# The sync engine reads the places of a pair of blocks ahead of its wait for their buffer, and the last sequence's results get buffers of their own

## The reference

```python
x = x + _layernorm(_L0_attn_ref(_layernorm(x), W_q, W_k, W_v, W_o))
x = x + _layernorm(_L0_ffn_ref(_layernorm(x), gate_w, gate_bias, Wg, Wu, Wd, Ws_g, Ws_u, Ws_d))

# in _L0_ffn_ref, x being its (normed) input:
hg = jnp.einsum('nh,eih->nei', xf, Wg)
hu = jnp.einsum('nh,eih->nei', xf, Wu)
act = jax.nn.silu(hg) * hu
y = jnp.einsum('nei,ne,ehi->nh', act, cw, Wd)      # cw: gates, 4 of 16 nonzero per token
shared = jax.nn.silu(xf @ Ws_g.T) * (xf @ Ws_u.T) @ Ws_d.T
return x + (y + shared)
```

## Time and profile before

| | us |
|---|---|
| median of 3 runs | 1031.69 (1030.8 to 1032.27) |
| the profiled execution | 1031.85 |
| its span | 1030.0 |
| TensorE busy | 830.4 (81%) |
| DVE busy | 654.9 (64%) |
| ACT busy | 452.2 (44%) |
| POOL busy | 434.8 (42%) |
| chain that ended last | PE 27%, DVE 12%, DMA 6%, issue 5%, SPq 4% |
| mean granted TensorE clock | 0.90 of full speed |

### The profile page before, as it was taken

One profiled execution on the slowest core, in us unless ns is written; L12 is line 12 of the kernel. 1 busy time (PEld: TensorE's weight loads), 2 busy tenths in 40 slices (PEclk: granted clock), 3 DMA queues, 4 the chain that ended last, 5 costly groups with the idle time before them and its releaser, 6 DMA issues.

```text
span 1030.0 us, 20612 instructions
## 1 busy us (share of the span) xinstructions
PE 830.4 (81%) x6580; PEld 610.5 (59%) x6580; DVE 654.9 (64%) x1906; ACT 452.2 (44%) x763; POOL 434.8 (42%) x416
## 2 busy tenths in 40 slices
PE   3449887896898798698796887799988999988763
PEld 3326454564565465466464555688877788777521
DVE  4375758687687787777777694554553333877543
ACT  2115544553544455363464555555444455444300
POOL 4431203115425425424522424467567655655610
PEclk9758989899898899898898898899999999998977
DMA  4475744334444443533559422354556667988663
GB/s 164 118 189 149 226 109 126 81 84 138 127 112 116 130 123 118 136 102 98 157 156 304 138 88 91 109 177 150 175 172 217 201 168 265 337 302 305 237 234 123
DMA packets 89175, 168.72 MB, mean 164 GB/s; under 512 B 14704, under 2 KB 56688, under 8 KB 88816
## 3 DMA queue, kind: packets, MB, share of 16 engines
q1 hardware_dynamic: 75248, 128.85, 43.7%
q0 software_dynamic: 13824, 38.55, 9.9%
HBM read 90.15 MB, written 76.68 MB: 162 GB/s over the span
## 4 chain that ended last, share of the span: by engine, by line
PE 27%; DVE 12%; DMA 6%; issue 5%; SPq 4%; POOL 3%; ACT 2%; DVEq 0%; ACTq 0%; POOLq 0%
PE ring L1480 7%; PE ring L1501 3%; DVE nmax L781 3%; DMA xg<-sorted_rows 2%; PE ring L1259 2%; DMA ykt<-expert_rows 2%; PE ring L1466 2%; PE ring L1261 2%; PE ring L1260 2%; POOL expert_rows L699 2%; PE ring L1380 2%; SPq L592 2%; PE ring L1337 1%; DMA expert_rows<-ys,dest 1%; SPq L593 1%
## 5 line engine op out<-in xcount | busy, mean ns | idle before, releaser
L1189 ACT ACTIVATE prob<-ring 128x1024 f32<-128x1024 f32 (+1 forms) x192 | 167.4, 880 | 208.1 <-PE ring L1328 207.8
L781 DVE TENSOR_REDUCE nmax<-ring 128x2 f32<-128x1024 f32 (+3 forms) x256 | 200.8, 818 | 43.5 <-PE ring L1310 41.6
L699 POOL DMA_INDIRECT expert_rows<-ys,dest x160 | 157.7, 985 | 96.9 <-ACT ys L1143 40.5
L691 POOL DMA_INDIRECT sorted_rows<-xr,idx_all x128 | 131.0, 1023 | 79.7 <-DVE xr L940 46.6
L1480 PE MATMUL ring<-we,xh 128*128 x640 | 155.1, 386 | 0.0
L1480 PEld LDWEIGHTS ring<-we,xh 128*128 128x128 f32 x640 | 118.3, 195 | 13.3
L1003 DVE SCALAR_TENSOR_TENSOR sl<-sl,got,ring 128x128 f32<-128x128 f32 x160 | 48.3, 344 | 104.1 <-ACT sl L1241 103.8
L1322 PE MATMUL ring<-maskt_b,halves_b 64*128 64x128 bf16 (+2 forms) x768 | 57.2, 229 | 63.6 <-DVE nmax L781 37.0
L669 POOL TENSOR_TENSOR rot<-rot 128x512 f32<-128x512 f32 x16 | 20.4, 1278 | 204.6 <-DVE rot L773 204.6
L1322 PEld LDWEIGHTS ring<-maskt_b,halves_b 64*128 64x128 bf16 x768 | 22.5, 96 | 133.2 <-DVE nmax L781 53.7
L1337 PE MATMUL ring<-prob,v_sb 128*32 128x512 f32 (+3 forms) x1024 | 97.9, 481 | 1.7 <-ACT prob L1189 1.7
(11 more groups left out here) (194 smaller groups left out, 1673.7 us busy)
## 6 DMA issues: line engine op xcount, KB each, us to landing
xg<-sorted_rows SPq DMA_DIRECT2D x160, 134.0 KB, 2.5
parts<-part SPq DMA_DIRECT2D x32, 512.0 KB, 5.8
ykt<-expert_rows SPq DMA_DIRECT2D x16, 1024.0 KB, 9.4
k_st<-parts SPq DMA_DIRECT2D x64, 128.0 KB, 3.6
q_st<-parts SPq DMA_DIRECT2D x64, 128.0 KB, 3.5
we<-w_exp SPq DMA_DIRECT2D x1, 6144.0 KB, 21.9
sorted_rows<-zeros SPq DMA_DIRECT2D x2, 2144.0 KB, 12.0
sorted_rows<-zeros SPq DMA_DIRECT2D x32, 134.0 KB
```

What stands on the lines that cost most here:

```text
L691: pool.indirect_dma_start(out=xs[group_of(s)], out_offset=bass.IndirectOffsetOnAxis(ap=idx_all[:, s, t, k:k + 1], axis=0), in_=xr[:, s % 2 ...
L699: pool.indirect_dma_start(out=yk, out_offset=bass.IndirectOffsetOnAxis(ap=dest[:, j % 8, b:b + 1], axis=0), in_=ys[:, j % NYS, b, :], in_o ...
L781: dve.tensor_reduce(nmax[:, Q % 2, :, pp, qb], slot[:, :, col:col + (qb + 1) * P], AX.X, ALU.max, negate=True).then_inc(s_max, 1)
L1189: act_e.activation(prob[:, u % 2, 2 * half:2 * half + 2, 0:width], slot[:, :, 0:width], ACT.Exp, scale=SCALE).then_inc(s_exp, 1)
```

## The change

Two things. In `load_block` both value loads of a pair come ahead of the waits for the buffer; the two loads of `xg` stay behind them. And the last sequence (7) gets places of its own, `ykt_last`, `zt_last` and `x1t_last`, in the space of `w_hi`, `w_lo`, `h_hi` and `h_lo`; semaphores are added for them. `home(s)` is the number of a sequence's place, `turn(s)` the how many-th use of it this is, `back(s)` gives its three tiles. In group 1 all residual loads (CZ 5, 6, 7) and then all six loads of parts (CL) come at the head of the steps.

```diff
@@ def sums(g)
     halves = [(s, h) for s in range(first, end) for h in range(2)]
+    if end == B:
+
+        steps = [("CZ", g, s) for s in range(first, end)] + [("CL", g, *half) for half in halves]
+        for i, (s, h) in enumerate(halves):
+            steps += [("CA", g, s, h), ("CS", g, s, h)]
+            if i:
+                steps.append(("CN", g, *halves[i - 1]))
+        return steps + [("CN", g, *halves[-1])]
@@ places
+        cursor[0] = w_low
+        ykt_last = place("ykt_last", [P, NT, TOPK, D])
+        zt_last = place("zt_last", [P, NT, D])
+        x1t_last = place("x1t_last", [P, NT, D])
+        assert cursor[0] <= w_high
@@ semaphores
-        s_cl = [sem(f"parts_back{i}") for i in range(4)]
-        s_cz = [sem(f"residuals_back{i}") for i in range(2)]
+        s_cl = [sem(f"parts_back{i}") for i in range(6)]
+        s_cz = [sem(f"residuals_back{i}") for i in range(3)]
-        s_out = [sem(f"out_stored{i}") for i in range(2)]
+        s_out = [sem(f"out_stored{i}") for i in range(3)]
@@ which place
+        def home(s):
+
+            return 2 if s == B - 1 else s % 2
+
+        def turn(s):
+
+            return 1 if s == B - 1 else s // 2 + 1
+
+        def back(s):
+
+            if s == B - 1:
+                return ykt_last, zt_last, x1t_last
+            return ykt[:, s % 2, :, :, :], zt[:, s % 2, :, :], x1t[:, s % 2, :, :]
@@ SP: load_block
+                row = [sp.value_load(tab[blk:blk + 1, g, 0:1], min_val=0, max_val=E * REGION + (DUMMIES - 1) * P)
+                       for blk in (2 * i, 2 * i + 1)]
                 if j >= NXG:
                     sp.wait_ge(s_t1, j - NXG + 1)
                     sp.wait_ge(s_dest, j - NXG + 1)
                 for b in range(2):
-                    blk = 2 * i + b
-                    row = sp.value_load(tab[blk:blk + 1, g, 0:1], min_val=0, max_val=E * REGION + (DUMMIES - 1) * P)
-                    sp.dma_start(xg[:, j % NXG, b, :], xs[g][bass.ds(row, P), :]).then_inc(s_xg[j % NXG], 16)
+                    sp.dma_start(xg[:, j % NXG, b, :], xs[g][bass.ds(row[b], P), :]).then_inc(s_xg[j % NXG], 16)
@@ SP: load_residuals, load_sums
-                if s >= 2:
-                    sp.wait_ge(s_out[s % 2], 32 * (s // 2))
+                _, z_home, x1_home = back(s)
+                if turn(s) > 1:
+                    sp.wait_ge(s_out[home(s)], 32 * (turn(s) - 1))
...
-                if s >= 2:
+                if turn(s) > 1:
                     sp.wait_ge(s_cn, N_OUT * (2 * (s - 2) + h + 1))
...
-                sp.dma_start(dst, per_token).then_inc(s_cl[2 * (s % 2) + h], 16)
+                dst = back(s)[0][:, NHALF * h:NHALF * h + NHALF, :, :].rearrange("p t k d -> p t (k d)")
+                sp.dma_start(dst, per_token).then_inc(s_cl[2 * home(s) + h], 16)
@@ PE: sum_results
-                pe.wait_ge(s_cl[2 * (s % 2) + h], 16 * (s // 2 + 1))
+                pe.wait_ge(s_cl[2 * home(s) + h], 16 * turn(s))
```

More of the change, by code:

```diff
@@ L590, in load_block @@
                 for b in range(2):
[L591 to L593 removed]
+                    sp.dma_start(xg[:, j % NXG, b, :], xs[g][bass.ds(row[b], P), :]).then_inc(s_xg[j % NXG], 16)
             def load_residuals(s):
[L596 to L597 removed]
+                _, z_home, x1_home = back(s)
+                if turn(s) > 1:
+                    sp.wait_ge(s_out[home(s)], 32 * (turn(s) - 1))
                 sp.wait_ge(s_zst, 16 * (s + 1))
                 sp.wait_ge(s_x1st, 16 * (s + 1))
[L600 to L601 removed]
+                sp.dma_start(z_home[:, :, :], packed(z_dram[s])).then_inc(s_cz[home(s)], 16)
+                sp.dma_start(x1_home[:, :, :], packed(x1_dram[s])).then_inc(s_cz[home(s)], 16)
             def load_sums(s, h):
@@ L617, in store_out @@
                 tiles = slice(NHALF * h, NHALF * h + NHALF)
-                sp.dma_start(rows(out[s])[:, tiles, :], zt[:, s % 2, tiles, :]).then_inc(s_out[s % 2], 16)
+                sp.dma_start(rows(out[s])[:, tiles, :], back(s)[1][:, tiles, :]).then_inc(s_out[home(s)], 16)
             load_x(0)
@@ L655, in _ @@
                     store_out(st[2], st[3])
-            for par in range(2):
-                sp.wait_ge(s_out[par], 32 * (B // 2))
+            for place_of in range(3):
+                sp.wait_ge(s_out[place_of], 32 * max(turn(s) for s in range(B) if home(s) == place_of))
         @block.gpsimd
@@ L1007, in final_sums @@
                 tiles = slice(NHALF * h, NHALF * h + NHALF)
-                y = ykt[:, s % 2, tiles, :, :]
+                y, z_home = back(s)[0][:, tiles, :, :], back(s)[1]
                 done = sums_before(s, h)
@@ L1011, in final_sums @@
                     if h == 0:
-                        dve.wait_ge(s_cz[s % 2], 32 * (s // 2 + 1))
+                        dve.wait_ge(s_cz[home(s)], 32 * turn(s))
                     n = 2 * (s - SHARED) + h
@@ L1031, in final_statistics @@
                 for t in range(NHALF * h, NHALF * h + NHALF):
-                    dve.bn_stats(st3[:, t, :], ykt[:, s % 2, t, 0, :]).then_inc(s_cst, 1)
+                    dve.bn_stats(st3[:, t, :], back(s)[0][:, t, 0, :]).then_inc(s_cst, 1)
                 for n in range(NHALF):
@@ L1044, in final_rows @@
                 dve.wait_ge(s_cr, 2 * s + h + 1)
+                y_home, z_home, x1_home = back(s)
                 for t in range(NHALF * h, NHALF * h + NHALF):
-                    dve.tensor_scalar(zt[:, s % 2, t, :], ykt[:, s % 2, t, 0, :], mv3[:, t, 0:1], rstd3[:, t:t + 1],
+                    dve.tensor_scalar(z_home[:, t, :], y_home[:, t, 0, :], mv3[:, t, 0:1], rstd3[:, t:t + 1],
                                       ALU.subtract, ALU.mult).then_inc(s_cn, 1)
                 dve.wait_ge(s_cn, done + NHALF)
-                dve.tensor_tensor(zt[:, s % 2, tiles, :], zt[:, s % 2, tiles, :], x1t[:, s % 2, tiles, :],
-                                  ALU.add).then_inc(s_cn, 1)
+                dve.tensor_tensor(z_home[:, tiles, :], z_home[:, tiles, :], x1_home[:, tiles, :], ALU.add).then_inc(s_cn, 1)
             dve.memset(zeros[:, :], 0.0).then_inc(s_init, 1)
@@ L1379, in sum_results @@
                 for k in range(TOPK):
-                    last = pe.matmul(ring[2][:, n % 2, :], ident, ykt[:, s % 2, NHALF * h:NHALF * h + NHALF, k, :],
+                    last = pe.matmul(ring[2][:, n % 2, :], ident, back(s)[0][:, NHALF * h:NHALF * h + NHALF, k, :],
                                      start=k == 0, stop=k == TOPK - 1)
```

5 lines of the change are left out of this document (3 added, 2 removed).

## The result

| | before | after |
|---|---|---|
| median of the runs, us | 1031.98 (1030.8 to 1033.94, 4 runs) | 1022.78 (1020.89 to 1023.75, 4 runs) |
| ratio after / before | | 0.9907, 95% interval 0.9885 to 0.9929 |
| profiled execution, us | 1031.85 | 1020.89 |
| its span, us | 1030.0 | 1019.1 |

The change saves 9.2 us of the medians, 0.9%. The forecast was 1020.8: 2 us too low, and inside its range.

The account below looks back on a forecast made before the run. The prediction saw the end bound by a detour for sequence 7, and SP late with xg pairs at two sites. Terms -1.15 - 1.2 - 10.0 + 1.5 = -10.85 gave a median of 1020.8 us, range 1018.0 to 1025.3.

Parts of the forecast that it names:

- The tail: Kernel's end: sequence 7's own home and six part loads in a row bring the last DVE sum 10.0 us sooner.
- The pads: Group 1's pads, 767 to 808: SP starts 1.15 us sooner, TensorE's xg stalls fall from 5.6 to 4.4; -1.15.
- the first sums: Behind the dest wait at 859.7: pairs and part loads come 1.15 us sooner, shortening DVE and TensorE waits; -1.2.
- Elsewhere 0: Remaining places, including TensorE's three xg waits in 860 to 980: the value loads gain nothing there; 0.
- three stalls of 9.3 us: TensorE's xg waits in 860 to 980, behind output stores or large loads: move along with what precedes them; 0.
- Rival 2: Value loads buy nothing: slower issues or growing later xg stalls take their gain; -8.5, 1023.2 us; chance 0.23.
- The residuals: Sequence 7's residual loads in the queue delay the scatter ahead of ACT's last ys write; +1.5, bounds 0 to 2.5.
- rival 1: Scatters get their turn among the loads, ACT's wait before the last ys stays 2.88; -12.4, 1019.3 us; chance 0.20.
- Rival 3: Tail's six loads share the engines and land together, first half +12.0; 1035.2 or 1032.8 us; chance 0.04.

Follow-up runs that it names:

- e11: Changed kernel with the last sequence's home but group 1's steps in the order of the kernel before; 1030.19 us, 0.9984 of the kernel before.
- e1: Kernel before with only the value loads moved ahead of the wait for dest; 1103.36 us, 1.0000 of the kernel before.
- e5: Changed kernel, group 0's residual loads, part loads and output stores issued behind the next pair's loads; 1074.09 us, 0.9882 of the kernel before.
- e8: Changed kernel, group 0's loads and stores behind the next pair, six group 1 pads before SP's long wait, others spread; 1013.18 us, 0.9793 of kernel before.
- e2: Changed kernel with the old load_block, so only the home and six part loads in a row; 1093.97 us, 0.9912 of the kernel before.
- e9: e8 with the value loads behind the wait again; 1015.59 us, 0.9829 of the kernel before.
- e3: Changed kernel with sequence 7's residual loads moved behind the six part loads; 1093.4 us, 0.9918 of the kernel before.
- e0: Changed kernel run again unaltered; 1096.08 us, 0.9932 of the kernel before on the same chip.
- b0: Kernel before run again unaltered, on another chip; 1085.43 us, 1.002 of the kernel before there.

## Why the prediction was right, and where it was wrong

**The tail, -10.0.** Right in size and mechanism: -9.9 in the pair of traces, -8.9 to -10.4 between any kernel with the home and the new order and any without both (27.55 to 28.80 against 37.65 to 37.97). 48 matmuls ran in one piece of 22.8 us (about 23 was forecast), the sixth sum came 1007.88 - 1001.01 = 6.87 after the fourth (some 7), and no part load follows the first output store. What was incomplete is the attribution: the forecast gave the waits for sequence 5's buffers equal rank with SP's order, and e11 shows that without these waits and with the old order only 0.5 us is won; the other 9.4 come with the new order, for which the home is needed.

**The pads, -1.15, and the first sums, -1.2.** Each came as read: 5.6 to 4.2 of stalls and -1.20 for the stage; DVE's wait for the first part 0.53 and TensorE's behind it 0.29 (forecast below 0.6 and below 0.4), -1.32 for the stage:

```profile
873.27 0.69 DVE L1052 TENSOR_TENSOR ykt<-ykt 128x512 f32<-128x512 f32 x1 [0.53 <-DMA ykt<-expert_rows]
878.48 0.44 PE L1526 MATMUL ring<-kc,sl 128*128 128x128 f32 x2 [0.29 <-DVE sl L1036]
```

**Elsewhere 0.** This is the step that failed. The forecast let the three stalls of 9.3 us "move along with what is before them". In the trace they took 2.9 us back, and e1 shows over 12 runs that the whole part is worth 0.0 within 0.2%. Two signs that the forecast had named failed with it: from the first write of `ys` to the last it took 300.6 us before and 300.8 after, where the block stage was to be 2.3 us shorter; and SP's waits for `dest`, which were to grow or stay in number, fell from 29 with 49.5 us to 21 with 38.3 us. What is shown: where the kernel before takes 1031 us the two sites gained 2.2 to 3.3 us in each of three traces, and by pair 79 nothing of it was left. What is argued only: that a pair early by 1.2 us meets a burst which is timed by something else, DVE's pace in the sums, and lands when the burst lets it. e5 and e8 support it, since without the burst in front of the pair those three stalls are gone and the ones of the next pairs are smaller. Against it stands e2: with the old value loads it had the longest three stalls of its chip, 12.0 us in total. The kernel that would measure the value loads without the bursts, e8 against e9, didn't settle it. Rival 2 foresaw this, as growth of just these stalls.

**The residuals, +1.5.** The mechanism was wrong, and rival 1 right: the scatter costs 0.2 more (0.5 by e3 and e0), not 1.5, and doesn't grow with the burst. The error was to read 6.08 against 2.38 as a queue whose length counts, and to put the 7.5 of another scatter on the same line, when both say only "under full engines".

**The sum.** -9.9 for the tail, 0 for the value loads, +0.2 for the scatter: -9.7, against 9.2 between the medians and 9.6 by the ratio. The forecast's -10.85 was near because two errors had opposite signs, 2.35 too much gain against 1.3 too much loss. Rival 2 at rival 1's scatter price, a case the forecast did not list, is -10.0: 1021.7. That the profiled execution, 1020.89, meets the forecast is chance: it started its experts 1.3 us sooner for reasons outside the change.

**Rival 3** (the loads share the engines) is refuted by the 4.90 us of the first load, which the trace before had already shown as 4.76 with four.

## What to carry to other kernels

A head start on a queue is worth what it is only up to the next thing that isn't moved with it: follow it to the end of the kernel, past every burst, and ask there what sets the moment. When a detour at the end has two causes, a shared buffer and an order of issue, take away one alone and see what remains; here a buffer of its own won 0.5 us in the old order and 9.9 with the new one, which it made possible. Before pricing a small transfer under a large one, take two bursts of different length, since a price that is a step and one that is a slope look alike in one row.

## What was not expected of the hardware

The last indirect scatters took 2.36 to 2.38 us when the burst was over and 5.7 to 6.3 under full DMA engines, with no growth from some 1 MB less to 2.1 MB more in the other queue; one issued at 922.17 before, under the loads for group 0's sums, took 7.5.

The kernel before took 1031 us on some chips and 1087 to 1104 on others. SP's register steps beside value loads, 18 and 152 ns in the median on all, took up to 0.7 and 1.4 us on the slower ones, 19 to 30 us in total in a run. That is not the whole of 56 to 72 us, and I don't know the rest. Much of it isn't in the experts' part at all: in b0 the first `ys` is written at 692.6, 16.5 us later than before.

TensorE's transposes behind a stall ran at the high clock after 2.14 and 2.87 us (0.66 and 0.69 for four) and at the low one after 3.12, 3.27, 3.85 and 4.54 (1.11 to 1.12), in the kernels before and after. Behind the one of 2.87 the granted clock then fell from 0.85 in the mean of 930.4 to 931.1 to 0.50 in 931.1 to 934.0, and the gate and up matmuls took 3.58. The length of the stall alone doesn't decide it: in e8 one of 3.29 left the clock high, in e3 one of 2.50 did not. Where it falls, the gate and up matmuls cost another 1.1 to 1.7 us (2.98 to 3.62 where the high clock gives 1.89).
